# Spreading the cumulative sums by DMA, and clamping the decay on VectorE, in a fused AdaLN, Mamba-2 and mixture-of-experts layer

## What is computed

```python
h = _layernorm(x) * (1 + ca) + sa
zxbcdt = h @ W_in                       # 256 -> 512 + 768 + 8
xBC = silu(causal_dwconv(xBC, 4 taps))
dt = softplus(dt + dt_bias);  dA = dt * -exp(A_log)
dA_cs = jnp.cumsum(dA, axis=2)          # within a chunk
diff = dA_cs[:, :, :, None, :] - dA_cs[:, :, None, :, :]
Lmat = jnp.where(causal, jnp.exp(diff), 0.0)
scores = jnp.einsum('bcihn,bcjhn->bcijh', Cc, Bc) * Lmat
y_diag = jnp.einsum('bcijh,bcjhp->bcihp', scores, xt)
... # states carried from chunk to chunk, y_off from them
y = rmsnorm((y_diag + y_off + x * D) * silu(z)) @ W_out;   x = x + ga * y
h = _layernorm(x) * (1 + cb) + sb
w = softmax(h @ gate_w + gate_b), those under 0.1 dropped, renormalized
x = x + gb * sum_e w[e] * (h @ expert_w[e] + expert_b[e])
```

## Time and profile before

| | us |
|---|---|
| median of 3 executions | 2381.42 |
| lowest, highest | 2378.87, 2386.04 |
| profiled execution, its own time | 2377.07 |
| its span | 2375.3 |

### The profile page before, as it was taken

The page is one execution under the profiler, slowest core; times in us unless marked ns, Lnnn a source line. Parts: engine busy times, 40 slices in busy tenths (PEclk is TensorE's granted clock), DMA queues, the critical chain, the costliest instruction groups (busy, mean ns, idle before and its releaser), DMA issues. The chain is left out here.

```text
span 2375.3 us, 48670 instructions
## 1 busy us (share of the span) xinstructions
PE 2284.0 (96%) x14936; PEld 1931.3 (81%) x14936; DVE 1805.0 (76%) x4070; ACT 1622.8 (68%) x4300; POOL 1561.3 (66%) x1812
## 2 busy tenths in 40 slices
PE   2589999999999999999999999999999999999997
PEld 2578888888888888888888888888888888888875
DVE  4378778877787877878877787787777888777763
ACT  1377777777777777777776777677777777677662
POOL 1156666767667766766676766676676767676685
PEclk6699999999999999999999999999999999999999
DMA  4000000000000000000000000000000000000000
GB/s 113 14 17 19 26 14 23 28 26 28 23 23 18 23 28 26 25 26 12 23 28 26 28 24 23 17 24 26 28 25 26 12 24 28 26 28 15 17 19 18
DMA packets 62926, 59.11 MB, mean 25 GB/s; under 512 B 10096, under 2 KB 62160, under 8 KB 62672
## 3 DMA queue, kind: packets, MB, share of 16 engines
q1 hardware_dynamic: 62672, 56.01, 7.5%
HBM read 39.22 MB, written 16.78 MB: 24 GB/s over the span
## 5 line engine op out<-in xcount | busy, mean ns | idle before, releaser
L858 DVE SCALAR_TENSOR_TENSOR feat<-pa,cw,feat 128x512 f32<-128x512 f32 x576 | 430.0, 746 | 65.9 <-ACT feat L547 55.3
L1163 PE MATMUL pe<-e_hi,h_hi 128*128 128x512 f32 x1024 | 447.1, 437 | 6.0 <-ACT eacc L682 2.5
L609 ACT ACTIVATE lm<-pd,e3in 128x128 f32<-128x128 f32 x1024 | 289.9, 381 | 198.5 <-PE pd L1163 195.0
L1163 PE MATMUL pe<-e_lo,h_hi 128*128 128x512 f32 x1024 | 405.9, 396 | 0.0
L1163 PE MATMUL pe<-e_hi,h_lo 128*128 128x512 f32 x1024 | 404.4, 395 | 0.0
L620 ACT ACTIVATE lm<-lm,lndt 128x128 f32<-128x128 f32 x1024 | 326.7, 401 | 0.1
L1048 DVE SCALAR_TENSOR_TENSOR eacc<-pe,wg,eacc 128x256 f32<-128x256 f32 x512 | 244.5, 478 | 63.6 <-PE pe L1163 54.4
L547 ACT ACTIVATE feat<-pa,cb,cw 128x512 f32<-128x512 f32 x192 | 151.0, 787 | 189.9 <-PE pa L1163 187.1
L1163 PE MATMUL pa<-h_hi,w_hi 128*128 128x260 f32 x768 | 235.6, 307 | 22.6 <-DVE feat L858 19.0
L429 POOL TENSOR_TENSOR ex<-ex 128x512 f32<-128x512 f32 x128 | 164.2, 1283 | 141.0 <-ACT ex L692 141.0
L1163 PE MATMUL py<-xt,mm 128*128 128x64 f32 x2048 | 253.7, 277 | 0.1
(11 more groups left out here) (173 smaller groups left out, 6332.3 us busy)
## 6 DMA issues: line engine op xcount, KB each, us to landing
xin<-_attn_hidden_states_dram SPq DMA_DIRECT2D x32, 512.0 KB, 3.9
xres<-_attn_hidden_states_dram SPq DMA_DIRECT2D x128, 128.0 KB, 2.5
out_dram<-x SPq DMA_DIRECT2D x128, 128.0 KB, 1.7
feat<-in_L_wmod_dram SPq DMA_DIRECT2D x1, 1536.0 KB, 6.7
feat<-in_L_attn_W_in_dram SPq DMA_DIRECT2D x1, 1024.0 KB, 5.9
gz<-in_L_ffn_expert_w_dram SPq DMA_DIRECT2D x1, 1024.0 KB, 9.0
x<-in_L_ffn_expert_w_dram SPq DMA_DIRECT2D x1, 1024.0 KB, 11.4
mm<-in_L_attn_W_out_dram SPq DMA_DIRECT2D x1, 512.0 KB, 6.9
```

Source lines behind the costliest of these rows:

```text
L609: last = act.activation(lm[:, h], pd[:, h // 4, h % 4 * P:(h % 4 + 1) * P], ACT.Relu, scale=-1.0, bias=e3in[:, x.q, 0, x.t, h:h + 1])
L858: dve.scalar_tensor_tensor(out=acc, in0=pa[:, :, 1 + j:1 + j + HT], scalar=cw[:, f, j:j + 1], in1=acc, op0=ALU.mult, op1=ALU.add).then_inc ...
L1163: return pe.matmul(o, lhsT=l, rhs=r, start=start, stop=stop, skip_group_check=True)
```

## The change

The three-part split, its transposes, the selection matmuls `D_` and the tiles `sel`, `identb`, `parts`, `csT` are gone. Instead, `cs_` has a third product, which gives cs with (tile, head) on 32 partitions and tokens along the row; ScalarE copies it to `csR`; SP stores it to a DRAM tensor of 16 KB per group (`put_cs`), and for each tile reads the eight rows back to all 128 partitions of `lm` (`load_L`, 512 KB written in SBUF). `lm` has two buffers now, one per parity of the tile, and `M_` works in it in place.

The decay becomes exp(min(cs_i - (cs_j - log dt_j), log dt_j)). VectorE does the subtraction and the min per head with two per-partition scalars (`decay`, four heads a step), and ScalarE one exponential over all eight heads. The exponential's table is wanted now at a point between the silus, and the instruction stream of ScalarE holds 128 table loads where 64 stood.

The logits are made of the split rows `h2_hi`, `h2_lo` and a split gate matrix `g_hl` (16 columns), into `pd` bank 1, and added up in two steps. The bias is one matmul of 512 columns for two tiles, copied into an `eacc` of four slots.

The order tables of all engines are new. The core of the diff:

```diff
+            def put_cs(sp, x):
+                sp.wait_ge(S["csTe"], x.g + 1)
+                sp.dma_start(cs_dram[x.g].rearrange("(r n) -> r n", n=P), csR[:]).then_inc(s_cs, 16)
+            def load_L(sp, x):
+                sp.wait_ge(s_cs, 16 * (x.g + 1))
+                if x.n >= 2:
+                    sp.wait_ge(S["ydiag"], x.n - 1)
+                rows = cs_dram[x.g:x.g + 1, x.t * NH * P:(x.t + 1) * NH * P]
+                sp.dma_start(lm[:, x.j].rearrange("p h n -> p (h n)"), rows.to_broadcast([P, NH * P])).then_inc(s_L[x.j], 16)
...
-                    for h in range(h0, h1):
-                        last = act.activation(lm[:, h], pd[:, h // 4, h % 4 * P:(h % 4 + 1) * P], ACT.Relu,
-                                              scale=-1.0, bias=e3in[:, x.q, 0, x.t, h:h + 1])
-                    for h in range(h0, h1):
-                        last = act.activation(lm[:, h], lm[:, h], ACT.Exp, scale=-1.0, bias=lndt[:, x.q, x.t, h:h + 1])
+            def Lx_(act, x):
+                use_table("natural_log_exp_and_others")
+                act.wait_ge(S["L"], 2 * (x.n + 1))
+                act.activation(lm[:, x.j], lm[:, x.j], ACT.Exp).then_inc(S["Lx"], 1)
...
+            def decay(h0, h1):
+                def step(dve, x):
+                    dve.wait_ge(s_L[x.j], 16 * (x.pair + 1))
+                    dve.wait_ge(S["es"], 3 * (x.g + 1))
+                    for h in range(h0, h1):
+                        last = dve.tensor_scalar(lm[:, x.j, h], lm[:, x.j, h], csl[:, x.q, x.t, h:h + 1], lndt[:, x.q, x.t, h:h + 1],
+                                                 ALU.subtract, ALU.min)
...
-                dve.tensor_tensor(mm[:], lm[:], rep(gs[:], NH, P), ALU.mult).then_inc(S["M"], 1)
+                dve.tensor_tensor(lm[:, x.j], lm[:, x.j], rep(gs[:], NH, P), ALU.mult).then_inc(S["M"], 1)
...
+                mm_(pa[0:T * NH, 1, 0:P], flat, tri[:], True, True).then_inc(S["cs"], 1)
...
-                for h in range(NH):
-                    last = mm_(pd[:, h // 4, h % 4 * P:(h % 4 + 1) * P], sel[:, h], csT[:, x.q, x.t], True, True)
...
-                        last = mm_(pd[:, 0, j * NE:(j + 1) * NE], h2f[:, k, j * P:(j + 1) * P], gate_f[:, k], k == 0, k == KT - 1)
+                        for i, h in enumerate((h2_hi, h2_lo)):
+                            last = mm_(pd[:, 1, 2 * j * NE:2 * (j + 1) * NE], h[:, x.pair % NH2, k, j * P:(j + 1) * P], g_hl[:, k],
+                                       k == 0 and i == 0, k == KT - 1 and i == 1)
...
-                mm_(pe_[:, 1, 0:DM], wgT[:], eb3[:, x.t], True, True).then_inc(S["bias"], 1)
+                mm_(pe_[:, 1], wgT[:], eb3[:, x.t:x.t + 2].rearrange("p t n -> p (t n)"), True, True).then_inc(S["bias"], 1)
...
                 do(cs_, pe, n - 4)
-                do(h2T_, pe, n - 8)
+                do(xT_, pe, n - 4)
```

608 lines of the change are left out of this document (279 added, 329 removed).

## The result

The changed kernel takes 2492.03 us (median, 2491.78 to 2497.28), the kernel before 2381.1 beside it: a ratio of 1.0468, 95% interval 1.0447 to 1.049. It is 4.7% slower. The prediction was 2329 us with a range of 2270 to 2450. The profiled execution's span is 2490.1 us.

A forecast was written before the change was run, and what follows sets the result against it. The prediction took TensorE to bound the kernel: 2377 - 94 us of TensorE work + 42 us of waits at group ends = 2325, with 4 us to the median some 2329 us; range 2270 to 2450.

The forecast's parts named there:

- TensorE's sum: TensorE's work: D_ -80, csT_ -10, bias -16, logits +3, cs_ +9, in all -94 us.
- wrong if TensorE's busy time falls by less than 80 us: Sign against the forecast, on TensorE's busy time; the other was idle above 90 us in the steady stretch.
- VectorE's sum: VectorE's total: 1805 + 261 (clamp) - 60 (parts_) + 16 (es_, lg_) + 113 (lock) = 2135 us.
- GpSimd's lock: VectorE and GpSimd hold one port pair in turn; 1024 new clamp instructions wait 0.11 us each, +113 us.
- The DMA way, hidden: Between cs_ and La: lm arrives 8.1 us after cs_, VectorE reaches La at 8.6, so the load is just hidden.
- The place: Group end, first tile's decay: M_ ends at 14.0 us, TensorE waits 1.3 us in each of 32 groups, 42 us.
- It fits, at 98%: Steady stretch: VectorE's 1850 us of work fit into 1888 us of TensorE work.
- VectorE becomes the bound, through GpSimd: Rival on VectorE's clamps: GpSimd's turns cost 0.25 us each, 256 us in place of 113; some 2460 us, chance 0.22.
- spread over taps, y4 and S_ instead: Sign that VectorE is the bound: TensorE's idle time spread over these steps.
- TensorE stays the only bound: Rival: the chain is shorter or its wait is caught up; 2287 us, chance 0.28.
- The round trip through DRAM: Rival: each microsecond lm lands after 8.6 us adds 32 us; 2377 at +1.5 us, 2425 at +3; chance 0.13.
- ScalarE, 0 us: ScalarE loses L609 (289.9 us), gains 135 us of exponentials and has air; zero cost on the path except inside the chain.

The follow-up runs named there:

- the emptiest run: Changed kernel with the clamp nearly left out, GpSimd's xd and y addition light, and most of y3, y4, M_ and the first expert addition left out: 2321.7 us.
- GpSimd lighter: Changed kernel with GpSimd's product xd and its addition to y on 64 of 512 columns: 2433.7 us, ratio 1.0209.
- The runs with a longer step there: Changed kernel with a mask on VectorE and eight exponentials on ScalarE, 2469.4 us; changed kernel with clamp and exponential per head on ScalarE, 2838.4 us.
- the clamp in fours: Changed kernel with two clamp instructions of four heads per tile in place of eight, one head's scalars for all four: 2385.8 us, ratio 1.0019.
- the run with the mask: Changed kernel with one VectorE addition of a -1e5 triangle in place of the clamp, and eight exponentials on ScalarE: 2469.4 us, ratio 1.0376.
- the clamp by halves: Changed kernel with the clamp as one subtraction and one min against 80 on 128x512, in La and again in Lb: 2516.5 us, ratio 1.0573.

## Why the prediction was wrong

**TensorE's sum, -94 us: too large.** The fastest period seen in the new order is 2.26 us a group below the old one, 66 us in 29 periods, and 61 by the four groups set side by side. D_ was taken at 80 us, the group's share of busy time; by distance it is 8.71 x 8 = 70 (the prediction had this value, 69, and passed over it), and taking matmuls away returned 0.053 us each. The bias was taken at 16: its group's 0.345 us counts time in which a neighbour's matmul also ran; by distance it is 8, and alone it brought 4. csT_ (10), the logits (+3, measured 0) and cs_ (+9, measured 11) were right. The sum of the parts is 78 us. That only 61 to 66 came is mostly idle time that is left even in the emptiest run (1.70 us in four groups, 14 in all), a wait for wg first. The prediction's own sign, "wrong if TensorE's busy time falls by less than 80 us", came true in full: it fell by nothing in the changed kernel and by 76 to 79 us only with VectorE and GpSimd out of the way (2208.3 and 2205.3 us).

**The filling of the pipeline, 0 us: missing.** 15 us in the emptiest run of the new order, 25 in the changed kernel.

**VectorE's sum: right.** 335 ns were forecast for the new instruction and the median is 337; the total was to be 2135 us and is 2104. The estimate of 0.22 us, from the tier table of the Trainium skill's "VectorE: DVE Perf Modes" with the per-partition scalars free, is too low: the shortest of the 1024 takes 313 ns. The measurement decides.

**GpSimd's lock, +113 us at 0.11 for each clamp: near in sum, wrong in place.** The clamp's mean is 56 ns above its median, 57 us, or 80 above its shortest, 82 us: half to three quarters of what was taken. xn, which the sum left alone, went from a mean of 416 to 903 ns, 62 us, and y4 from 812 to 696, 15 us less. That these add up to about 113 is luck. With GpSimd lighter VectorE is 104 us less busy. Whom it hits seems to matter more than how much: xn stands directly ahead of transposes of TensorE, whose wait for it (14.3 us) goes when GpSimd is light.

**The DMA way, hidden: right.** La begins 8.5 us after cs_ (8.6 forecast), and the load costs VectorE 4.1 us in all. That small stores and loads beside the broadcasts land later (an out row in 4.0 us, 1.7 in the earlier trace rows) was not foreseen. GpSimd waits 26.0 us for such a load (xres) in the steady stretch; whether this costs time wasn't tested.

**The place, 42 us: near enough there, wrong as the whole.** The chain was forecast to end M_ at 14.0 us; it ends at 13.4. TensorE was forecast to wait 1.3 us; it waits 0.75 in the group shown and 23.1 us in 27 waits, 0.86 each. The step that failed is "It fits, at 98%. That is little room, and it is why I look for the place where the order makes TensorE wait". It treated VectorE's room as one sum and its lateness as one place, and so priced all that VectorE's and GpSimd's work does to TensorE at 42 us. In the changed kernel VectorE is only 89% busy in the steady stretch and TensorE 96%, and TensorE waits for it in up to six places per group while it waits for TensorE in others. Taking 250 us of the clamp's work away from VectorE, which had 11% of its time free in the steady stretch, brought 116 us, nearly half; making GpSimd light brought 44 to 58. Together 160 us of span (2490.1 to 2329.9), where the prediction had 42.

**Rivals.** "VectorE becomes the bound, through GpSimd" (2460 us, 0.22) was the nearest, and its sign, idle time "spread over taps, y4 and S_ instead", is what the waits show, with lm, xn, feat, y and wg in the list. Its price was wrong: 0.25 us for each clamp was never paid, and neither is VectorE the bound by its sum. The rival's own sum is off too: 2329 + 143 is 2472, not 2460, and of the 143 us some 38 would have fitted into the room that 98% left. "TensorE stays the only bound" came out at 2321.7 and not 2287 in the run nearest to it. The round trip through DRAM costs VectorE 4.1 us of waiting in the new order; in the old one the kernel with it is 284 us slower than the one before.

**ScalarE, 0 us: nothing here speaks against it, but the reason given (room) doesn't hold.** The runs with a longer step there lost up to 84 and 346 us with ScalarE at 58 and 61%.

The clock has a share, which the prediction left out. Behind the wait ahead of ydiag_ at 1352 us:

```profile
1350.00:1352.00 2.00, 1.26 (x10) 1.07 (x9) 2.00 (x5) 1.39 (x3) 1.04 (x1) 1.00 0.00 0
1352.00:1354.50 2.50, 2.49 (x17) 2.49 (x18) 2.46 (x8) 0.00 (x0) 0.86 (x1) 0.73 0.00 0
1354.50:1356.00 1.50, 1.50 (x7) 1.40 (x8) 1.50 (x6) 0.41 (x1) 0.00 (x0) 0.50 0.02 5
```

TensorE was busy 1.26 of 2 us, and then the granted clock (third column from the end) fell to 0.50, which is 1.2 GHz. In the steady stretch it averages 0.988 over twenty equal slices, against 0.996 before and 1.00 in the runs with the clamp in fours and without it. Over 1970 us that is an estimate of 16 us of the loss against the kernel before, and of 24 of the 116 us of the clamp. At this place the fall stands behind a wait; which waits bring it isn't shown, for the run with the mask has 87 us of visible waits in the stretch and a clock of 1.00.

What stays open: which of the three differences lengthens the second and third group, which waits lower the clock, and why the clamp by halves is 24 us slower with the same total on VectorE. A correct clamp that costs VectorE as little as the run in fours wasn't found.
